# A GNN kernel whose scattered start rows get a small array for the first 14 chunks and the large array within the loop

## What is computed

```python
def _node_proj(x, W, b, node_type):            # 2 node types
    p = einsum('nf,tfh->tnh', x, W) + b[:, None, :]
    return take_along_axis(p, node_type[None, :, None], axis=0)[0]
h1, h2, h3, h4 = (_node_proj(x, W, b, node_type) for W, b in ...)
w5e = einsum('mf,mfh->mh', edge_feat, W5[edge_type]) + b5[edge_type]
num = sum(h3[edge_dst] * (h4[edge_src] + w5e), axis=-1)
score = softmax((num / sqrt(16.0))[:, None], axis=-1)[:, 0]
out0 = h1 + segment_sum(score[:, None] * (h2[edge_src] + w5e), edge_dst)
x = layernorm(x + out0)
m = relu(x[src] + (edge_feats @ We + be)) + 1e-7     # layer 1
a = softmax of m over the edges of one destination
x = layernorm(x + (x + segment_sum(m * a, dst)) @ Wm + bm)
```

## Time and profile before

| | |
|---|---|
| median of three runs | 2248.02 us |
| lowest, highest | 2237.88, 2254.48 us |
| profiled execution | 2247.74 us |
| its span, first to last instruction | 2245.8 us |
| outside the span | 1.9 us |
| mean granted clock of TensorE | 0.886 of full |
| busy: PE / DVE / ACT / POOL | 1747.1 / 1602.6 / 757.1 / 1294.3 us |
| moved by DMAs | 323.65 MB |

### The profile page before, as it was taken

The page is one execution under the profiler, slowest core; times in us unless marked ns, Lnnn a source line. Parts: engine busy times, 40 slices in busy tenths (PEclk is TensorE's granted clock), DMA queues, the critical chain, the costliest instruction groups (busy, mean ns, idle before and its releaser), DMA issues.

```text
span 2245.8 us, 29209 instructions
## 1 busy us (share of the span) xinstructions
PE 1747.1 (78%) x9112; PEld 1108.5 (49%) x9112; DVE 1602.6 (71%) x3058; ACT 757.1 (34%) x1397; POOL 1294.3 (58%) x1348
## 2 busy tenths in 40 slices
PE   6453889898889889888873487888878787878873
PEld 5222556665666556555662144454445444544442
DVE  7422677777777777677768377788778786878786
ACT  3100222222222222222222144455455545455461
POOL 6365555555666565565633666666666665656624
PEclk9876999999999999999986688899999998989885
DMA  8942444545554555454443145555545555545442
GB/s 274 369 96 83 131 137 134 156 134 154 138 150 141 144 145 144 137 146 133 139 133 93 39 117 148 148 161 153 148 147 150 150 148 143 152 144 151 144 151 57
DMA packets 220072, 323.65 MB, mean 144 GB/s; under 512 B 62802, under 2 KB 127948, under 8 KB 219789
## 3 DMA queue, kind: packets, MB, share of 16 engines
q1 hardware_dynamic: 132958, 150.94, 22.9%
q0 software_dynamic: 43056, 68.05, 13.7%
q10 hardware_dynamic: 43904, 102.79, 12.6%
HBM read 188.35 MB, written 133.22 MB: 143 GB/s over the span
## 4 chain that ended last, share of the span: by engine, by line
PE 28%; issue 17%; another core or an unknown queue 16%; ACT 12%; DVE 12%; ACTq 3%; POOL 2%; DMA 1%; DVEq 0%; SPq 0%; POOLq 0%
PE wide L957 8%; PE wide L1069 5%; ACT block L860 3%; PE wide L931 3%; PE wide L966 2%; ACTq L853 2%; ACT prob_wide L837 2%; PE wide L923 2%; ACT msg L838 2%; ACT block L841 1%; DVE h3d L1363 1%; PE bank L1005 1%; ACT block L830 1%; DVE featm L1354 1%
## 5 line engine op out<-in xcount | busy, mean ns | idle before, releaser
L672 POOL DMA_INDIRECT rows<-d_x,idx x588 | 559.7, 952 | 350.2 <-issue 155.3
L662 POOL DMA_INDIRECT block<-d_h,idx x482 | 462.9, 960 | 302.9 <-issue 126.8
L1069 PE MATMUL wide<-late,ntype_i 125*128 125x512 bf16 x975 | 240.4, 404 | 54.7 <-DVE ntype_i L1492 49.5
L662 POOL DMA_INDIRECT rows<-d_h,idx x160 | 153.8, 961 | 151.6 <-PE wide L931 58.3
L1363 DVE TENSOR_TENSOR_SCAN h3d<-keep,h3d,bank 128x512 f32<-128x512 bf16 x98 | 124.9, 1275 | 159.1 <-issue 114.4
L1069 PE MATMUL wide<-edge_lists,ntype_i 125*128 125x512 bf16 x936 | 229.2, 401 | 11.9 <-issue 11.5
L931 PE MATMUL wide<-typed,zeros 128*128 128x128 f32 (+1 forms) x1364 | 185.0, 283 | 13.1 <-issue 13.1
L1080 PE MATMUL wide<-ident,block 128*128 128x128 f32 x784 | 134.4, 320 | 72.0 <-ACT block L860 43.9
L1069 PEld LDWEIGHTS wide<-late,ntype_i 125*128 125x128 bf16 x975 | 101.1, 104 | 176.2 <-DVE ntype_i L1492 49.9
L957 PE MATMUL wide<-late,ntype_i 125*128 125x512 bf16 x702 | 177.1, 409 | 12.5 <-issue 5.0
L957 PE MATMUL wide<-edge_lists,ntype_i 125*128 125x512 bf16 (+1 forms) x702 | 170.7, 396 | 11.6 <-issue 9.2
(11 more groups left out here) (255 smaller groups left out, 3214.2 us busy)
## 6 DMA issues: line engine op xcount, KB each, us to landing
d_run<-block ACTq DMA_DIRECT2D x98, 512.0 KB
d_inj<-zeros SPq DMA_DIRECT2D x28, 896.0 KB
inj<-d_inj SPq DMA_DIRECT2D x98, 256.0 KB
d_run<-stage ACTq DMA_DIRECT2D x98, 256.0 KB
feat<-in_ea16x3T SPq DMA_DIRECT2D x196, 96.0 KB
types<-d_type SPq DMA_DIRECT2D x196, 64.0 KB
keep<-d_keep SPq DMA_DIRECT2D x196, 64.0 KB
keep<-d_pen SPq DMA_DIRECT2D x196, 64.0 KB
```

What stands on the lines that cost most here:

```text
L662: pool.indirect_dma_start(out=ring[c % RING][:, j, h, :], out_offset=None, in_=d_h24, in_offset=bass.IndirectOffsetOnAxis(ap=idx[:, c, at: ...
L672: pool.indirect_dma_start(out=rows1[c % RING1][:, j, h, :], out_offset=None, in_=d_x1, in_offset=bass.IndirectOffsetOnAxis(ap=idx[:, c, at ...
L1069: ins = pe.matmul(p_hot[s], table[q][:, SPLIT * k:SPLIT * (k + 1), :].rearrange("p b c -> p (b c)"), hot[s][:, k, :], start=(k == 0 and q ...
```

## The change

The injected rows of the first 14 chunks go to an array of their own, d_early, with 14336 rows and dump rows behind. It is cleared by 4 units; d_inj's units 0 to 3 are not cleared, since nothing reads them, and its other 24 units are cleared 3, 4 and 3 in the head, and 14 within the loop, 2 after each of the chunks 2 to 8. A clearing DMA now reads 448 columns of zeros four times instead of 1792 columns once. DVE makes a second index list early_i (5 more small operations ahead of the release of POOL). POOL first scatters into d_early, then gathers chunks 0 to 10, then waits for the 24 clearing units and scatters all nodes into d_inj, then gathers on. Chunk 14 is the first that loads from d_inj. Two units instead of four are picked ahead of the loop, and pieces start in step 0. Waits on other steps are dropped on POOL (L649 to L656, L683) and on SP and ACT (for the clearing). On DVE the split of x into tables moves behind the index lists. On SP load_pick stands ahead of load_features0 in its iteration.

```diff
-AHEAD = 6
 ZEROS = 28
-ZEROS_EARLY = 7
+ZEROS_EARLY = 3
+ZEROS_LATE = 14
+EARLY = 14
+EARLY_UNITS = 4
+EARLY_ROWS = EARLY * 2 * CH
+SCATTER_BEHIND = 10
-PICK_LEAD = 4
+PICK_LEAD = 2
-FIRST_STEP = 3
+FIRST_STEP = 0
@@ block.sync @@
+            no_rows = zeros[:, 0:7 * C].unsqueeze(1).to_broadcast([P, 4, 7 * C])
+            def clear(first, behind):
+                for z in range(first, behind):
+                    sp.dma_start(flat[z], no_rows).then_inc(s_injzero, 16)
-            for z in range(ZEROS_EARLY):
-                sp.dma_start(flat[z], zeros[:, :]).then_inc(s_injzero, 16)
+            for z in range(EARLY_UNITS):
+                sp.dma_start(flat_early[z], no_rows).then_inc(s_early, 16)
+            clear(EARLY_UNITS, EARLY_UNITS + ZEROS_EARLY)
...
-            def load_inj(s, r, of_inj):
+            def load_inj(s, r, c):
                 wait(sp, injT[s], r)
-                sp.dma_start(inj[s][:, :, :], d_inj[bass.ds(of_inj, 2 * CH), :]
+                if c == EARLY:
+                    sp.wait_ge(s_inj, 2 * 16 * NT)
+                sp.dma_start(inj[s][:, :, :], (d_early if c < EARLY else d_inj)[bass.ds(c * (2 * CH), 2 * CH), :]
...
-            sp.wait_ge(s_injzero, 16 * ZEROS)
...
             for c in range(2, CHUNKS):
                 s, r = c % 2, c // 2
-                load_features0(s, r, halves(c))
-                load_inj(s, r, c * (2 * CH))
-                load_keep(s, r, halves(c))
                 for u in range(PICK_LEAD + 1, UNITS):
                     if c == max(2, UNTIL[u - LISTS] + 1):
                         load_pick(u)
+                load_features0(s, r, halves(c))
+                load_inj(s, r, c)
+                load_keep(s, r, halves(c))
+                clear(min(ZEROS_LATE + 2 * (c - 2), ZEROS), min(ZEROS_LATE + 2 * (c - 1), ZEROS))
@@ block.gpsimd @@
+            pool.wait_ge(s_sel, KT)
+            pool.wait_ge(s_early, 16 * EARLY_UNITS)
+            pool.wait_ge(s_rows_i, 1)
+            scatter(d_early, early_i)
             pool.wait_ge(s_h24, 16 * 6)
-            for c in range(AHEAD):
-                gather0(c)
-            pool.wait_ge(s_injzero, 16 * ZEROS)
...
+            for c in range(CHUNKS):
+                gather0(c)
+                if c == SCATTER_BEHIND:
+                    pool.wait_ge(s_injzero, 16 * (ZEROS - EARLY_UNITS))
+                    pool.wait_ge(s_inj, 16 * NT)
+                    scatter(d_inj, first_i)
@@ block.scalar, ahead of typed_w @@
-            act.wait_ge(s_injzero, 16 * ZEROS)
+            act.wait_ge(s_zeros, 1)
```

More of the change, by code:

```diff
@@ L114, in gnn_program @@
         d_inj = scratch("d_inj", [EP + P * NT, C])
+        d_early = scratch("d_early", [EARLY_ROWS + P * NT, C])
         d_run0 = scratch("d_run0", [EP + 1, C])
@@ L177, in gnn_program @@
         first_i = sb("first_i", [P, NT], i32)
+        early_i = sb("early_i", [P, NT], i32)
         mid_i = sb("mid_i", [NP, 2], i32)
@@ L451, in _ @@
             sp.dma_start(idx[:, 0:RING, :], all_idx[:, 0:RING, :]).then_inc(s_idx[0], 16)
-            flat = d_inj[0:EP, :].rearrange("(z p r) c -> z p (r c)", z=ZEROS, p=P)
+            flat, flat_early = (rows.rearrange("(z p a x) c -> z p a (x c)", z=units, p=P, a=4)
+                                for rows, units in ((d_inj[0:EP, :], ZEROS), (d_early[0:EARLY_ROWS, :], EARLY_UNITS)))
+            no_rows = zeros[:, 0:7 * C].unsqueeze(1).to_broadcast([P, 4, 7 * C])
+            def clear(first, behind):
+                for z in range(first, behind):
+                    sp.dma_start(flat[z], no_rows).then_inc(s_injzero, 16)
             sp.dma_start(x_sb[:, :, :], t["x"].rearrange("(p i) c -> p i c", i=NT)).then_inc(s_types, 16)
@@ L490, in _ @@
             sp.dma_start(wm[C:P, :], t["ident"][C:P, C:P]).then_inc(s_weights, 16)
-            for first, behind, zeroed, zeros_to in ((0, 10, ZEROS_EARLY, 11), (10, 20, 11, 14), (20, NT, 14, ZEROS)):
+            for first, behind, zeroed, zeros_to in ((0, 10, EARLY_UNITS + ZEROS_EARLY, 11), (10, 20, 11, ZEROS_LATE), (20, NT, ZEROS_LATE, ZEROS_LATE)):
                 sp.wait_ge(s_sel, (behind + 1) // 2)
@@ L494, in _ @@
                     sp.dma_start(of_node[a:b, first:behind, :], H[a:b, first:behind, C:3 * C]).then_inc(s_h24, 16)
-                for z in range(zeroed, zeros_to):
-                    sp.dma_start(flat[z], zeros[:, :]).then_inc(s_injzero, 16)
+                clear(zeroed, zeros_to)
             def load_features0(s, r, of_edge):
@@ L1180, in _ @@
             then(dve.tensor_scalar(first_i[:, :], node_i[:, :], float(DUMP), None, ALU.add))
+            then(dve.tensor_scalar(early_i[:, :], node_i[:, :], float(EARLY_ROWS), None, ALU.add))
             dve.wait_ge(s_edges, 64)
@@ L1250, in _ @@
             for i in range(NT):
-                if i == BOUNDS[3]:
-                    for q in range(3):
-                        then(dve.memset(table[q][:, NT:, :], 0.0))
-                    dve.wait_ge(s_rounded, 1)
-                    dve.tensor_tensor(left0, x_sb[:, :, :], table[0][:, 0:NT, :], ALU.subtract).then_inc(s_left, 1)
                 dve.wait_ge(s_got[group_of(i)], 16 * size(group_of(i)))
@@ L1270, in _ @@
             dve.wait_ge(s_mbcol, 1)
-            dve.wait_ge(s_rounded, 2)
-            dve.tensor_tensor(table[2][:, 0:NT, :], left0, table[1][:, 0:NT, :], ALU.subtract).then_inc(s_left, 1)
+            for q in range(3):
+                then(dve.memset(table[q][:, NT:, :], 0.0))
             dve.wait_ge(s_shift, 1)
@@ L1281, in _ @@
             then(dve.tensor_tensor(tmp_n[:, :], tmp_n[:, :], in_row[:, :], ALU.add))
-            dve.tensor_copy(first_i[0:NP, :], tmp_n[:, :]).then_inc(s_rows_i, 1)
+            then(dve.tensor_scalar(in_row[:, :], tmp_n[:, :], float(EARLY_ROWS), None, ALU.is_lt))
+            dve.tensor_copy(first_i[0:NP, :], tmp_n[:, :])
+            then(dve.scalar_tensor_tensor(tmp_n[:, :], tmp_n[:, :], float(-EARLY_ROWS), node[:, :], ALU.add, ALU.subtract))
+            then(dve.tensor_tensor(tmp_n[:, :], tmp_n[:, :], in_row[:, :], ALU.mult))
+            then(dve.scalar_tensor_tensor(tmp_n[:, :], tmp_n[:, :], float(EARLY_ROWS), node[:, :], ALU.add, ALU.add))
+            dve.tensor_copy(early_i[0:NP, :], tmp_n[:, :]).then_inc(s_rows_i, 1)
+            dve.wait_ge(s_rounded, 1)
+            dve.tensor_tensor(left0, x_sb[:, :, :], table[0][:, 0:NT, :], ALU.subtract).then_inc(s_left, 1)
             dve.wait_ge(s_h3, 1)
```

28 lines of the change are left out of this document (9 added, 19 removed).

## The result

The changed kernel takes 2414.37 us (median of 3 runs, 2409.62 to 2421.85) against 2248.02 before: a ratio of 1.075, 95% interval 1.067 to 1.083, so 7.5% slower. The forecast of 2219 us, and its range up to 2285, are wrong.

The account below looks back on a forecast made before the run. Bound by a head of some 203 us where PE mostly waits, then a PE-bound layer 0 loop with DVE close behind. 71 - 12 - 30 = 29 us off 2247.74 gave 2219 us, range 2184 to 2285.

Parts of the forecast that it names:

- 71 us won at chunk 11: Head: chunk 11's scan at 245 us instead of 316.35, by the chain of scatters and gathers on POOL.
- rival 4: Head: unexplained 15.6 us before the first scan recur, chunk 11 at 258, 13 us less gain; no separate chance given.
- the unexplained stall: Head before the change: 187.2 to 202.8 us, ahead of the first scan, without a cause in the profile; 15.6 us.
- stalls before chunk 11 hide in POOL's time: Head: clearing's DMA load and late features before chunk 11 are covered by POOL's time; uncovered, they add their full amount.
- the clearing behind keep: Head: last two clearing units stand behind keep of chunk 8, landing near 196 us; the second scatter waits, +6 us.
- The dropped waits: POOL, SP and ACT: removing these waits costs nothing, since ring and index waits stay.
- The mask's wait: Loop, DVE: mask stands 4.1 us for late features at 28 places behind chunk 11.
- 1.05 each: Loop: late masks' net cost per place after PE's result lag; 28 places, 30 us.
- rival 2: Loop: DVE's 4.1 us stall passes whole into the next scan at 28 places, 115 us, 2304 us total; chance 0.18.
- PE's lag: Loop: PE's results come 2.1 us (median) behind its rows; if work still in the array, it soaks up late masks.
- Pieces at the end: Loop end: steps 91 to 93 get pieces, costing 12 us, bounds 5 and 14.

Follow-up runs that it names:

- the lists behind keep: Changed kernel with load_pick moved back behind the keep loads of its iteration: 1891.46 us, against 1906.08 for the kernel before.
- the paced kernel: Changed kernel with waits added in front of POOL's gathers of chunks 2 to 7: 2071.1 us, and 2067.77 when run again.
- the chunk-later run: Changed kernel with load_pick still ahead of the features, but issued one chunk later, when its wait has long been met: 1897.31 us.

## Why the prediction was wrong, point by point

**The head.** The steps on POOL hold: first scatter 65.8 (65.2), its end 103.1 (101.4 with the load of idx). The first scan, put at 112, comes at 116.3 to 119.5 on the later chips. Chunk 11, put at 245, comes at 244.85 with the lists behind keep, by the chain on POOL that the prediction gave. On the first chip it comes at 385.9. The step that failed there is "71 us won at chunk 11". In the sum this gain carries no late result of PE at all, and rival 4 lets the unexplained stall come again at its old size, "13 us less". It came three times, for some 145 us in all between 100 and 372 (43 and 39 in the head, and 72 instead of 10 between two scans). It had been in the profile before, in the line with "remote", and I gave it a small price because it had a small size, though I had no mechanism that bounds it. The same sum leans on 316.35 for chunk 11 before; on the later chips, without that stall and the late results in the steps behind it, that is 277.1, and the gain at chunk 11 is 32 us (277.1 to 244.9), not 71.

A second step failed on the later chips: "stalls before chunk 11 hide in POOL's time". With the lists ahead chunk 11 comes at 259.9, 15 us later. The late features also delay the clearing behind keep, and the scatter waits for it; POOL's row in the changed kernel on chip 12:

```profile
213.29 1.00 POOL L684 DMA_INDIRECT d_inj<-H,first_i  x1 [13.78 <-DMA d_inj<-zeros]
```

With the lists behind keep this row starts at 198.22, 15 us earlier.

**The dropped waits** ("cost nothing"). On the later chips so: without them the kernel before takes 1902.8 and 1904.6 us in two runs. For the first chip it stays open. In the trace of the changed kernel there the long stalls begin where POOL issues without pause (65.8 to 173 and 276 to 358 us), but such a run of POOL exists on a later chip too (66.5 to 199.5 us), without the stall, so it is not a sufficient cause; the run that would tell, the paced kernel on the first chip, was not to be had.

**load_pick.** The cause, the 28 places and the wait's engine were as the prediction had them; the size was not. The mask's wait was put at 4.1 us and is 5.2 to 5.3. The issues were right: the last feature DMA stands 2.9 us behind the list's issue (627.74 to 630.65), put at 1.1 + 1.75. But from there to use it took 4.2 (630.65 to 634.83), not 2.84, a figure read from a load of inj in the head; the 2.2 us that the prediction gave beside it is further off still. The step that failed is "1.05 each", which took the wait of PE place by place, less the 2.1 us by which its results are late. The changed kernel on a later chip loses 163.5 us from chunk 11 to 91 against the one with the lists behind, 5.8 us a place: DVE's stall passes whole, 5.2 a place, and the rest is the longer wait for PE's look-up. That is rival 2, with 5.8 for its 4.1. On the first chip this stretch lost 101 us, 3.6 a place. Some of it is not the lists' (on the later chips 17 us, 740.3 against 722.9), so an estimate for them is (101 - 17) / 28 = 3.0 a place, of a mask wait of 5.3. That PE's late results soak up the rest there was argued in the prediction and is not shown; for it speaks that the median by which the inj turn's semaphore comes behind its row falls from 2.7 us to 1.3 with the change. The price was too low in either case, because the wait was netted against PE's lag alone, and an idle time of 1.23 us ahead of one scan was taken to speak against rival 2, while from the mask on everything in DVE's order, and PE's projection, stands behind it. The sentence of the Trainium skill (DMA: Bandwidth & Descriptors, Anatomy of one DMA), that a wait is served on the issuing sequencer before dispatch, was the right warning, and the runs agree with it: the unmet wait held back the four issues behind it, and with the wait met the same order costs 6 us instead of 175 (1897.3 and 2066.5 against 1891.5).

**The end.** Pieces at the end were put at 12 us; by chunks 87 to 97 they cost 8.2 on the later chips (74.5 less 66.3). The clearing behind keep was put at 6 us: POOL waits 3.4 us for it on a later chip with the lists behind, 13.8 with them ahead, and 50.4 on the first chip, where its chunks were late.

**The sum on a later chip**, with measured terms: 32 won at chunk 11, some 8 lost at the end, 10 more in the loop without a cause shown (9.29 against 9.15 us a chunk from 11 to 87; of 320 to 950 us DVE stands idle for 7.4 us ahead of 8 scans, for 0.9 ahead of one in the kernel before, marked "issue"), which leaves the 14 us of the kernel with the lists behind; then 175 lost with the lists ahead (2066.5 less 1891.5), 163.5 in the loop and 15 ahead of chunk 11 in the profiled executions, which are 181 apart. On these chips the rest of the change was worth having, and the move of three lines beside it cost some ten times as much. For the first chip no run tells the two apart.

## What to carry to other kernels

A load with an unmet wait in a queue has the price of everything behind it, not its own: put it last, or issue it when the wait is long met (the chunk-later run gave back 169 of 175 us by one index). Do not let an engine's idle time at one place absorb a stall of a fixed order on another engine unless a run shows that it does; take the whole stall as the middle case. And an unexplained stall in a profile is an unknown with no upper bound by its size: the head's gain should have carried it in the range.

## What the runs showed of the hardware

The same kernel took 2248 us in the first measurement and 1904 to 1912 on the four chips of the later ones. The number of the first chip is not known, so whether the chip or its state at the time makes the difference is open. One stretch of layer 1, 1400 to 1800 us, the kernel before: on the first chip, then on a later one (window, length, busy us of each engine, PEclk, DMA share, GB/s):

```profile
1400.00:1800.00 400.00, 333.47 (x1606) 189.91 (x1604) 321.79 (x570) 205.47 (x355) 247.43 (x262) 0.92 0.52 152
```
```profile
1400.00:1800.00 400.00, 372.20 (x1956) 216.26 (x1956) 396.28 (x692) 249.52 (x431) 302.54 (x320) 1.00 0.63 185
```

DVE gets 81% of its work done in the same time, and its instructions last as long on both (a scan 1.28 us), so its own pace is not the difference. The granted clock is 0.92 against 1.00, and a matmul row lasts 0.208 us in the mean against 0.190 (333.47 / 1606, 372.20 / 1956). That is 9% where PE gets done 18% less, so the clock is at most a part of it, and it may as well follow from PE's idle time. What differs besides is when PE's results count as there. In the loop of layer 0 the semaphore of the inj turn (L983) comes 2.7 us behind the end of PE's row in the median on the first chip, 0.01 us on the later one; for the look-up of L949 in the head of the changed kernel on the first chip it was 43 us. Why, the traces do not tell, and how much of the 342 us this makes is not shown. For such a comparison the kernel before has to be run on the same chip, as it was for all runs here.
